# Mixture-of-experts kernel: token rows turned by 128-byte transfers and VectorE blocks, not by TensorE

## The reference

```
x = layernorm(x + attention(x))                        # 16 heads of 16 features
# mixture of experts, 8 experts, 2 per token, capacity ceil(4096*2/8*1.25) = 1280 rows each
gates = softmax(x @ gating_w);  topk_w, topk_idx = top_k(gates, 2)
buf[e, slot] = x[token]                                # rows beyond the capacity are dropped
h     = relu(buf[e] @ w1[e] + b1[e])                   # 256 -> 1024
out_e = h @ w2[e] + b2[e]                              # 1024 -> 256
y[token] += weight * out_e[slot]
x = layernorm(x + y)
```

## Time and profile before

| | |
|---|---|
| median of 3 runs | 818.93 us (818.16 to 819.34) |
| the profiled execution's own time | 819.39 us |
| its span, first to last instruction | 817.7 us |
| TensorE busy | 771.9 us, 94% of the span |
| VectorE, ScalarE, GpSimd busy | 605.5, 442.8, 403.4 us (74%, 54%, 49%) |
| bytes moved, small packets | 94.35 MB; 10924 of 71534 packets under 512 B |

### The profile page before, as it was taken

The page is one execution under the profiler, slowest core; times in us unless marked ns, Lnnn a source line. Parts: engine busy times, 40 slices in busy tenths (PEclk is TensorE's granted clock), DMA queues, the critical chain, the costliest instruction groups (busy, mean ns, idle before and its releaser), DMA issues.

```text
span 817.7 us, 16633 instructions
## 1 busy us (share of the span) xinstructions
PE 771.9 (94%) x5919; PEld 644.4 (79%) x5919; DVE 605.5 (74%) x1325; ACT 442.8 (54%) x753; POOL 403.4 (49%) x599
## 2 busy tenths in 40 slices
PE   7789999999999988889999999999999999999993
PEld 6567777777777755778898898888988988988993
DVE  6657888889888898968657568568568567575982
ACT  3156777777777767645345345345445344444670
POOL 1000166665565547764364464463552553546774
PEclk9689999999999999999999999999999999999998
DMA  5567776565555682443352452452441633434841
GB/s 160 119 158 168 173 167 137 138 149 122 121 123 110 126 197 64 160 147 81 83 106 44 97 110 40 97 110 40 101 107 30 150 53 78 103 52 66 316 167 48
DMA packets 71534, 94.35 MB, mean 115 GB/s; under 512 B 10924, under 2 KB 55885, under 8 KB 71324
## 3 DMA queue, kind: packets, MB, share of 16 engines
q1 hardware_dynamic: 53308, 69.10, 32.1%
q0 software_dynamic: 16928, 22.61, 15.6%
q10 hardware_dynamic: 1216, 1.57, 0.9%
HBM read 39.76 MB, written 27.92 MB: 83 GB/s over the span
## 4 chain that ended last, share of the span: by engine, by line
PE 76%; DVE 12%; issue 4%; POOL 3%; DMA 3%; ACTq 0%; ACT 0%; POOLq 0%; DVEq 0%; SPq 0%
PE bank L1723 15%; PE bank L990 11%; DVE negm L895 10%; PE wide L1692 8%; PE wide L1691 8%; PE wide L1690 8%; PE bank L1725 8%; PE wide L1035 7%; PE bank L1669 2%; PE wide L1053 2%; PE bank L999 2%; PE bank L1100 1%; POOL slot_list L538 1%; DMA stack<-qk 1%; POOL out L1420 1%
## 5 line engine op out<-in xcount | busy, mean ns | idle before, releaser
L1364 POOL DMA_INDIRECT acc_rows<-o_w,lists x70 | 116.8, 1668 | 178.7 <-ACT o_w L1513 165.3
L895 DVE TENSOR_REDUCE negm<-wide 128x4 f32<-128x1024 f32 x128 | 156.1, 1222 | 36.8 <-PE wide L1035 36.7
L635 ACT ACTIVATE probs<-wide 128x1024 f32<-128x1024 f32 x128 | 131.0, 1024 | 61.8 <-PE wide L1053 60.2
L1480 ACT ACTIVATE h<-wide,b1T 128x512 f32<-128x512 f32 (+1 forms) x200 | 115.3, 601 | 89.2 <-PE wide L1692 65.2
L1725 PE MATMUL bank<-stack,h_lo 128*128 128x256 f32 x560 | 156.7, 280 | 0.0
L1690 PE MATMUL wide<-g_hi,stack 128*128 128x512 f32 (+1 forms) x400 | 139.4, 349 | 0.9 <-ACT h L1480 0.7
L1692 PE MATMUL wide<-g_hi,stack 128*128 128x512 f32 (+1 forms) x400 | 139.1, 348 | 0.0
L1691 PE MATMUL wide<-g_lo,stack 128*128 128x512 f32 (+1 forms) x400 | 138.9, 347 | 0.0
L1513 ACT ACTIVATE o_w<-o_b,lists 128x256 f32<-128x256 f32 x70 | 35.7, 510 | 147.5 <-DVE o_b L1651 147.5
L1723 PE MATMUL bank<-stack,h_hi 128*128 128x512 f32 x304 | 108.0, 399 | 1.6 <-DVE o_b L1651 1.6
L1725 PEld LDWEIGHTS bank<-stack,h_lo 128*128 128x128 f32 x560 | 105.9, 189 | 0.0
(11 more groups left out here) (212 smaller groups left out, 1637.9 us busy)
## 6 DMA issues: line engine op xcount, KB each, us to landing
stack<-qk SPq DMA_DIRECT2D x180, 128.0 KB, 3.9
w_raw<-in_L_ffn_w SPq DMA_DIRECT2D x16, 1024.0 KB, 5.9
x_sb<-in_L_attn_x SPq DMA_DIRECT2D x16, 256.0 KB, 4.7
x_rows<-x SPq DMA_DIRECT2D x16, 256.0 KB, 3.6
acc_rows<-x SPq DMA_DIRECT2D x16, 256.0 KB, 4.1
acc_sb<-acc_rows SPq DMA_DIRECT2D x8, 512.0 KB, 8.3
out<-acc_sb SPq DMA_DIRECT2D x8, 512.0 KB, 2.6
x_rows<-zrow SPq DMA_DIRECT2D x2, 1152.0 KB, 6.6
```

Of the source, the lines that this page charges most:

```text
L635: nc.scalar.activation(probs[:, i % 4].rearrange("p x c t -> p x (c t)"), shifted_banks(i)[:, :, :], ACT.Exp, scale=SCALE).then_inc(exp_do ...
L895: nc.vector.tensor_reduce(negm[n % 2][:, :, :, u].rearrange("p c x -> p x c"), score_banks(PAIRS * n + u)[:, :, :].rearrange("p x (c t) -> ...
L1364: nc.gpsimd.indirect_dma_start(out=acc_d, out_offset=bass.IndirectOffsetOnAxis(ap=lists[:, e, QC * c + r, 0:1], axis=0), in_=o_w[c][:, r, ...
L1480: ins = nc.scalar.activation(h[u % 2][:, t], banks[BZ[u % 4]][:, t], ACT.Relu, bias=b1T[:, FT * e + f:FT * e + f + 1])
```

## The change

From the second expert on (e > 0) TensorE turns no rows. SP copies a super's gathered rows inside SBUF into a buffer `shuffled`, in 16 transfers per super: each takes a block of 32 partitions and puts its columns of 32 floats (128 bytes) into another quarter of the partitions, so that the 32x32 blocks stand where the turned matrix wants them. Two buffers serve the supers by turns. VectorE turns every 32x32 block of a chunk in one instruction (`turn`, 128x512 float32) into `turned_rows` (two buffers, by chunk). ScalarE writes the high part from there (`rows_hi`), GpSimd the low part (`rows_lo`: 128x512, two SBUF inputs), where VectorE did it from PSUM before.

Around it: GpSimd gathers six chunks ahead, not five; `take_in` of chunks 0 and 1 stands after five of the eight units of `third`, chunk 2 amid the next `first`, and chunks 3 and 4 between layer2 of chunks 3 and 4 of the expert before (for the last expert after its `second`, as before). SP's list per expert is now: w2, shuffle of `first`, shuffle of `second`, the next w1, shuffle of `third`. GpSimd's list has the low parts between its gathers and add-backs, and those of the last expert's chunks 2, 3 and 4 ahead of gather_sums. Half of the final rows' buffer moves into the weights' raw buffers, a few semaphores are shared, and two of them renamed. The core of the diff:

```diff
-    AHEAD = 5
+    AHEAD = 6
+    BLOCK = 32
+    QUARTERS = P // BLOCK
+    MOVES = QUARTERS * QUARTERS
+    IN_WEIGHTS = 2
...
-        rows = [sb(f"rows{c}", [P, QC, D]) for c in range(2)]
+        rows_first = sb("rows_first", [P, 2, QC, D])
...
+        rows_third = sb("rows_third", [P, 2, QC, D])
+        rows_of = (rows_first, rows_second, rows_third)
+        rows = [rows_of[s][:, i] for s, cs in enumerate(SUPERS) for i in range(len(cs))]
...
-        a = sb("acc_sb", [P, NG, GROUP, D])
+        acc_sb = sb("acc_sb", [P, NG - 2 * IN_WEIGHTS, GROUP, D])
+        shuffled = [sb(f"shuffled{i}", [P, PAIR, QC * DK, QUARTERS, BLOCK]) for i in range(2)]
+        turned_rows = [sb(f"turned{i}", [P, QC * DK, P]) for i in range(2)]
+        moved = [sem(f"moved{i}") for i in range(2)]
+        turned = sem("turned")
...
+        def moved_count(e, s):
+
+            return 16 * MOVES * ((super_no(e, s) - len(SUPERS)) // 2 + 1)
+
+        def turned_view(e, c):
+
+            return turned_rows[(NC * e + c) % 2][:, :, :].rearrange("p (r k) t -> p k r t", k=DK)
+
+        def chunk_view(t, e, c):
+
+            s, off = of_chunk(c)
+            return t[super_no(e, s) % 2][:, :, off:off + C].rearrange("p k (r t) -> p k r t", r=QC)
...
         def sync_program(sp):
-            for e in range(1, NE):
-                sp.wait_ge(gT_ready, NC * (e - 1) + 3)
+            def load_w1(e):
                 sp.wait_ge(w1_hi_done, PARTS * e)
                 sp.wait_ge(w1_lo_done, PARTS * e)
                 sp.dma_start(w1_raw[:, :, :], w1_d[e].rearrange("(c p) f -> p c f", p=P)).then_inc(w1_loaded, 16)
+
+            def load_w2(e):
                 sp.wait_ge(w2_hi_done, PARTS * e)
                 sp.wait_ge(w2_lo_done, PARTS * e)
                 sp.dma_start(w2_raw[:, :, :], w2_d[e].rearrange("(f p) d -> p f d", p=P)).then_inc(w2_loaded, 16)
+
+            def shuffle(e, s):
+                i, count = super_no(e, s), len(SUPERS[s])
+                for c in SUPERS[s]:
+                    sp.wait_ge(gathered[c], 16 * QC * (e + 1))
+                if i >= len(SUPERS) + 2:
+                    e_, s_ = divmod(i - 2, len(SUPERS))
+                    sp.wait_ge(turned, NC * (e_ - 1) + SUPERS[s_][-1] + 1)
+                src = rows_of[s][:, :, :, :].rearrange("p c r (k q b) -> p (c r k) q b", q=QUARTERS, b=BLOCK)
+                dst = shuffled[i % 2][:, 0:count].rearrange("p c x t b -> p (c x) t b")
+                for q, t in itertools.product(range(QUARTERS), repeat=2):
+                    sp.dma_start(dst[q * BLOCK:(q + 1) * BLOCK, :, t, :], src[t * BLOCK:(t + 1) * BLOCK, :, q, :]).then_inc(moved[i % 2], 16)
+
+            sp.wait_ge(gT_ready, 3)
+            load_w1(1)
+            for e in range(1, NE):
+                load_w2(e)
+                shuffle(e, 0)
+                shuffle(e, 1)
+                if e + 1 < NE:
+                    load_w1(e + 1)
+                shuffle(e, 2)
+            sp.wait_ge(w1_hi_done, PARTS * NE)
...
+            def rows_free(e, c):
+
+                if e == 0:
+                    pool.wait_ge(gT_ready, c + 1)
+                elif e > 0:
+                    s = of_chunk(c)[0]
+                    pool.wait_ge(moved[super_no(e, s) % 2], moved_count(e, s))
+
             def gather(e, c):
 
-                n = NC * e + c
-                if n >= NC:
-                    pool.wait_ge(gT_ready, n - NC + 1)
+                rows_free(e - 1, c)
...
+            for c in range(EC, NC):
+                gather(0, c)
             pool.wait_ge(lists_loaded, 16)
             pool.wait_ge(late_loaded, 16)
+            for n in range(NC, AHEAD):
+                gather(n // NC, n % NC)
...
+            def rows_lo(e, chunks):
+                for c in chunks:
+                    pool.wait_ge(g_hi_done, NC * e + c + 1)
+                    nc.gpsimd.tensor_tensor(chunk_view(g_lo, e, c), turned_view(e, c), chunk_view(g_hi, e, c).bitcast(F32),
+                                            ALU.subtract).then_inc(g_lo_done, 1)
+
             for n in range(NC * LASTE):
+                e, c = divmod(n, NC)
                 if n + AHEAD < NE * NC:
                     gather((n + AHEAD) // NC, (n + AHEAD) % NC)
-                add_back(n // NC, n % NC)
+                if c == 2:
+                    rows_lo(e + 1, (0, 1))
+                if c == 3 and e + 1 < LASTE:
+                    rows_lo(e + 1, (2,))
+                add_back(e, c)
+                if c == 3 and e + 1 < LASTE:
+                    rows_lo(e + 1, (3, 4))
+            rows_lo(LASTE, (2, 3, 4))
...
                 i = super_no(e, s)
-                act.wait_ge(gT_ready, NC * e + c + 1)
                 if i >= 2:
                     act.wait_ge(z_ready, unit_no(*divmod(i - 1, len(SUPERS)), 0, None))
+                if e > 0:
+                    act.wait_ge(turned, NC * (e - 1) + c + 1)
+                    nc.scalar.activation(chunk_view(g_hi, e, c), turned_view(e, c), ACT.Copy).then_inc(g_hi_done, 1)
+                    return
+                act.wait_ge(gT_ready, c + 1)
                 nc.scalar.activation(g_hi[i % 2][:, :, off:off + C], bank(rows_bank(e, c), a=DK), ACT.Copy).then_inc(g_hi_done, 1)
 
...
+            def turn(e, c):
+                s, off = of_chunk(c)
+                i, n = super_no(e, s), NC * (e - 1) + c
+                dve.wait_ge(moved[i % 2], moved_count(e, s))
+                if n >= 2:
+                    dve.wait_ge(g_hi_done, NC + n - 1)
+                    dve.wait_ge(g_lo_done, NC + n - 1)
+                nc.vector.transpose(turned_rows[(NC * e + c) % 2][:, :, :].rearrange("p x t -> p (x t)"),
+                                    shuffled[i % 2][:, off // C].rearrange("p x t b -> p (x t b)")).then_inc(turned, 1)
+
+            def take_in(e, chunks):
+                if e > 0:
+                    for c in chunks:
+                        turn(e, c)
+                    return
+                for c in chunks:
+                    rows_lo(e, c)
...
@@ -1743,36 +1850,44 @@
         if e == 0:
             layer2(0, 0)
             layer2(0, 1, (0,))
-            take_in(0, 2)
+            take_in(0, (2,))
             layer2(0, 1, (1,))
             layer1(0, second, (0, 1))
-            take_in(0, 3)
-            take_in(0, 4)
+            take_in(0, (3,))
+            take_in(0, (4,))
             layer1(0, second, (2, 3))
         else:
             layer1(e, second)
-            take_in(e, 3)
-            take_in(e, 4)
+            if last:
+                take_in(e, (3, 4))
             layer2(e, 0)
             layer2(e, 1)
-        layer1(e, third)
-        if not last:
-            take_in(e + 1, 0)
-            take_in(e + 1, 1)
-            if split_w1:
-                split_w1(e + 1)
+        if last:
+            layer1(e, third)
+            layer2(e, 2)
+            layer2(e, 3)
+            layer2(e, 4)
+            return
+        layer1(e, third, range(5))
+        take_in(e + 1, (0, 1))
+        layer1(e, third, range(5, 8))
+        if split_w1:
+            split_w1(e + 1)
         layer2(e, 2)
         if e + 1 < NE - 1:
-            layer1(e + 1, first)
-            take_in(e + 1, 2)
+            layer1(e + 1, first, range(4))
+            take_in(e + 1, (2,))
+            layer1(e + 1, first, range(4, 8))
         layer2(e, 3)
+        if e + 1 < NE - 1:
+            take_in(e + 1, (3, 4))
         layer2(e, 4)
-        if not last and split_w2:
+        if split_w2:
             split_w2(e + 1)
         if e + 1 == NE - 1:
-            layer1(e + 1, first, (0, 1, 2, 3))
-            take_in(e + 1, 2)
-            layer1(e + 1, first, (4, 5, 6, 7))
+            layer1(e + 1, first, range(4))
+            take_in(e + 1, (2,))
+            layer1(e + 1, first, range(4, 8))
 
 
 
```

## The result

The changed kernel takes 857.88 us (median of 4; 855.44 to 858.99), the kernel before 819.13 beside it on the same chip: a ratio of 1.0467, 95% interval 1.0438 to 1.0496. Slower was forecast, but 826 us with a range up to 842. The profiled execution has a span of 857.2 us against the 825.6 of the sum: 31.6 us to be found.

What follows compares the result with a forecast made beforehand. TensorE was taken to bound the expert stage, and GpSimd's order as much as TensorE the end. Span 817.7 - 13.95 (transposes) + 13 (end) + 8.8 (ring) = 825.6, plus 1.2 to the median, rounded to 826 us; range 814.5 to 842.

Steps and rivals of the forecast that it cites:

- Removed transposes, 13.95: TensorE, up to its last layer2 of e = 6: six experts' transposes at 2.18 us and one pair at 0.87 gone.
- Durations of the added instructions: Per chunk: VectorE's block turn 0.69 us, ScalarE's copy 0.69, GpSimd's subtraction 1.28.
- The shuffle: SP's 16 transfers inside SBUF: 15 x 0.64 + 2.6 us of landing, 12.2 us; bounds 8 and 14.7.
- The ring: Waits from one expert's third shuffle to the next's through SP, GpSimd and VectorE: 57.3 us against TensorE's work of 55.55.
- five passes, 8.8 us: First third shuffle to the sixth: five passes, each costing 57.3 - 55.55 us, 8.8 us in all.
- the way of the gathers: GpSimd, before the next expert's first shuffle: two gathers, two add-backs, another gather and 2.9 of landing, 10.9 us.
- The end, 13 us: Last expert: low parts ahead of gather_sums make it 15.9 us late, put_rows 13 us late; bounds 10 and 15.
- Low parts as a step of the ring, 3.9: After the third shuffle lands: VectorE's turn, ScalarE's copy and two GpSimd low parts, 0.69 + 0.69 + 2 x 1.28 us.
- The bounds of the ring, 49 to 62: Ring length in us with the shuffle's bounds: at 49 TensorE sets the pace at no cost, at 62 it costs 32.
- No ring: Rival: SP issues transfers in 0.55 us or less, TensorE stays full, the end takes all back: 818 us, chance 0.28.
- GpSimd's end shorter: Rival: with the ring hidden, GpSimd's list from gather_sums to put_rows takes 3 us less: 815 us, chance 0.14.
- Dear pieces: Rival: a 128-byte piece costs three times 17 ns, so shuffle 15.7 us, ring 64.3, time 862; chance 0.08.

Runs made afterwards that it cites:

- sixteen_long_pieces: Changed kernel with 16 transfers per shuffle kept, but pieces of 1 KB and 512 bytes instead of 128 bytes: 851.84 us.
- the thirty-two: Changed kernel with each shuffle cut into 32 transfers of half the length instead of 16, same 128-byte pieces: 996.27 us.

## Why the prediction was wrong

- **Removed transposes, 13.95: right.** 2.1 us per expert, once nothing stands in their place.
- **Durations of the added instructions: right**, within 0.06 us each. The shuffle, forecast as 12.2 us, has a mean of 12.6 (third) and 13.2 (first).
- **The ring as mechanism: right.** Undone by gathers further ahead or fewer transfers, grown by 20.1 us with 32 transfers (there by way of all three shuffles).
- **The ring's length, 57.3, and the term "five passes, 8.8 us": the step that failed.** It is 60.8, and 5 x (60.8 - 57.3) = 17.5 us of the 31.6 are this. The 3.5 us lie in the two shuffles (1.4), in the h_lo of 1.67 us (1.0), for which the sum held nothing, in the way of the gathers (0.8, of it 0.5 in landings of 3.4 us on average where the median of before, 2.9, was taken), and in the low parts (0.3).
- **The number of passes.** The first expert and the sixth pass were taken to be free. w2's first load comes at 421.83 instead of 416.96 - 2.2 = 414.8, 7.1 us late, and the sixth pass holds what is left up to TensorE's last layer2 of e = 6, which is 770.88 - 742.1 = 28.78 us later than forecast: 28.78 - 7.1 - 17.5 = 4.2. TensorE's record of these 4.2 is its wait of 4.1 us, up to 757.78, for VectorE's bias, which stands behind the turn of the last expert's `first` (747.74): the ring's first half, once more.
- **The end, 13 us: the mechanism right, the size 15.9** (86.32 - 70.43 us from that layer2 to the end of the span), the remaining 2.9. The first gather_sums came 17.5 us late, not 15.9. I let GpSimd's list take back 2.9 us up to put_rows, 1.21 of it idle time; it took back 17.5 - 16.3 = 1.2. Its own work took back 3.0, but its wait ahead of put_rows, for the stores of the groups, grew from 1.21 to 2.93 us.
- **Low parts as a step of the ring, 3.9: half right.** They are on the chain, but a second branch, 1.8 us shorter in the kernel that takes them away, stands beside them, which the working of that step did not look for.
- **The range.** The bounds of the ring, 49 to 62, held the measured 60.8, which by the prediction's own sum gives 818 + 5 x 5.25 = 844; the range, up to 842, left that end out, for want of a reason why it should be reached. On average five of the six links came out longer and none shorter, since each was taken at the median or undisturbed value.
- **Rivals.** "No ring" and "GpSimd's end shorter" did not occur, and the kernel that opens the ring and frees the end shows what they needed. "Dear pieces" gave 862, near the time, by a cause that sixteen_long_pieces refutes.

## What to carry to other kernels

When work is taken off the busy engine and handed through queues of three others, draw the way from one turn of the loop to the next through every in-order queue, add it up with disturbed durations (the upper part of a row's spread, not its median), and look for a second branch before counting on the removal of one. If the ring is near the work's own length, open it (start loads further ahead) rather than shorten its links. An engine's idle share is no room if what it does delays a queue behind it, or slows an instruction of another engine.

## What the runs showed of the hardware

- A short wait of TensorE can cost more than its length. The changed kernel waits 3.01 us up to 573.33; in the next stretches the granted clock (the third number from the end) is:

```profile
573.33 0.47 PE L1794 MATMUL wide<-g_hi,stack 128*128 128x512 f32 x1 [3.01 <-issue]
```

```profile
574.00:576.00 2.00, 2.00 (x7) 1.54 (x6) 1.88 (x5) 0.52 (x2) 0.00 (x0) 0.59 0.35 38
576.00:578.00 2.00, 2.00 (x7) 1.54 (x6) 0.86 (x2) 1.07 (x2) 1.62 (x1) 0.56 0.85 338
578.00:580.00 2.00, 2.00 (x10) 1.67 (x9) 1.47 (x3) 1.25 (x2) 1.59 (x1) 1.00 0.85 231
```

  near 1.2 GHz for 4 us, then 2.4 again. That is 2 x (1 - 0.59) + 2 x (1 - 0.56) = 1.7 us of lost work behind a wait of 3.0, and TensorE's waits as listed then understate what the ring takes from it: 55.63 + 3.0 + 1.7 = 60.3 of a pass of 60.5. It is not so after every wait: of the six ahead of layer1 of `first` the clock fell after four (1.95 to 3.01 us long) and stayed at 1.00 after the first two (3.73 us up to 391.89, 2.78 us up to 452.38).
- SP issued copies of 32 partitions inside SBUF one every 0.63 to 0.73 us in the change, the long pieces and the thirty-two, whatever their pieces or bytes; four copies over all 128 partitions took 0.7 each in the burst shown.
- GpSimd's subtraction beside VectorE's: VectorE's 0.69 became 1.67 us (568.31 to 569.98; GpSimd's two low parts end at 569.42), GpSimd's own stayed at 1.33 on average. The Trainium skill's "GPSIMD Engine Reference" (Specifications) says that the two share their way into SBUF. The trace agrees, and here it is VectorE that paid.
- The prediction called the stretch of GpSimd's 0.23 us a quieter one. VectorE was busy through all of it, with row statistics that read one SBUF tensor; beside the 0.97 us it ran h_lo, which reads two (764.46 to 765.15). The kernel before:

```profile
769.58 7.47 DVE L1564 BATCH_NORM_STATS2 stats<-acc_sb 128x6 f32<-128x512 f32 x12
```

- VectorE's block transpose of 128x512 f32 took 0.69 us, the same as its subtraction of that shape.
